# Second attention: the exchange of the rotation's halves moves from two extra projections to a VectorE shuffle

## The reference, cut to what matters

```
def _apply_rope(x, cos, sin):
    d2 = x.shape[-1] // 2
    x1, x2 = (x[..., :d2], x[..., d2:])
    return jnp.concatenate([x1 * cos - x2 * sin, x2 * cos + x1 * sin], axis=-1)
qkv = x @ Wqkv.T + bqkv
qkv = qkv.reshape(b, t, 3, NHEAD, HEAD_DIM).transpose(2, 0, 3, 1, 4)
q, k, v = (qkv[0], qkv[1], qkv[2])
q = _apply_rope(q, cos, sin)
k = _apply_rope(k, cos, sin)
attn = jax.nn.softmax(jnp.einsum('bhqd,bhkd->bhqk', q, k) / scale, axis=-1)
out = jnp.einsum('bhqk,bhkd->bhqd', attn, v)
return out.transpose(0, 2, 1, 3).reshape(b, t, d) @ Wout.T + bout
```

## Time and profile before

| | |
|---|---|
| time, median of 3 runs (lowest to highest) | 2202.04 us (2201.79 to 2204.19) |
| span of the profiled execution, first to last instruction | 2190.9 us |
| busy, share of the span: PE, DVE, ACT, POOL | 73%, 57%, 49%, 37% |
| second attention, first statistics to last pick | about 1396 to 1914 us of the span |

### The profile page before, as it was taken

The page is one execution under the profiler, slowest core; times in us unless marked ns, Lnnn a source line. Parts: engine busy times, 40 slices in busy tenths (PEclk is TensorE's granted clock), DMA queues, the critical chain, the costliest instruction groups (busy, mean ns, idle before and its releaser), DMA issues. The chain is left out here.

```text
span 2190.9 us, 25810 instructions
## 1 busy us (share of the span) xinstructions
PE 1588.8 (73%) x8422; PEld 824.9 (38%) x8422; DVE 1256.8 (57%) x2743; ACT 1080.2 (49%) x2160; POOL 819.4 (37%) x1482
## 2 busy tenths in 40 slices
PE   2799999963498851615530179159999999879998
PEld 1133333312365640513430157013333333357776
DVE  3688888856434230154468721368777778435443
ACT  1377777755333330246650022217777776645554
POOL 3455554325334235270061776533344431012111
PEclk8699999985655555857755579559999999979999
DMA  3211212100000021100003113211111111010000
GB/s 97 73 66 61 70 67 67 45 1 1 1 1 1 1 81 51 30 7 1 0 3 116 39 39 28 49 72 55 57 57 58 60 52 52 12 40 10 6 10 15
DMA packets 85097, 85.19 MB, mean 39 GB/s; under 512 B 36070, under 2 KB 67664, under 8 KB 84836
## 3 DMA queue, kind: packets, MB, share of 16 engines
q1 hardware_dynamic: 75044, 76.43, 10.5%
q0 software_dynamic: 7680, 6.06, 1.7%
q10 hardware_dynamic: 2240, 1.05, 0.2%
HBM read 59.78 MB, written 25.17 MB: 39 GB/s over the span
## 5 line engine op out<-in xcount | busy, mean ns | idle before, releaser
L921 DVE TENSOR_REDUCE arena<-psum 128x2 f32<-128x1024 f32 x512 | 602.1, 1218 | 131.1 <-PE psum L720 126.4
L836 ACT ACTIVATE arena<-psum 128x512 f32<-128x512 f32 x1024 | 554.1, 595 | 141.0 <-PE psum L733 131.9
L733 PE MATMUL psum<-arena 99*128 99x512 bf16 x1024 | 312.6, 387 | 16.4 <-DMA arena<-arena 11.8
L720 PE MATMUL psum<-arena 72*128 72x512 bf16 x1024 | 287.5, 397 | 43.0 <-POOL arena L622 20.8
L743 PE MATMUL psum<-arena 128*32 128x512 f32 x2048 | 274.3, 608 | 3.0 <-ACT arena L836 1.9
L733 PEld LDWEIGHTS psum<-arena 99*128 99x128 bf16 x1024 | 74.8, 98 | 294.0 <-ACT arena L836 224.7
L720 PEld LDWEIGHTS psum<-arena 72*128 72x128 bf16 x1024 | 96.7, 102 | 185.6 <-DVE arena L921 28.5
L2406 ACT ACTIVATE arena<-arena 128x128 f32<-128x128 f32 x252 | 102.5, 482 | 110.5 <-POOL arena L2394 110.5
L2389 POOL TENSOR_SCALAR arena<-arena 128x4 f32<-128x4 f32 x80 | 22.3, 278 | 307.5 <-DVE arena L2383 302.7
L631 POOL TENSOR_TENSOR arena<-arena 128x16 bf16<-128x16 f32 x64 | 13.8, 216 | 317.6 <-DVE arena L921 223.3
L344 ACT ACTIVATE arena<-arena 128x128 f32<-128x128 f32 x192 | 76.7, 482 | 96.2 <-POOL arena L260 70.9
(11 more groups left out here) (436 smaller groups left out, 2647.6 us busy)
## 6 DMA issues: line engine op xcount, KB each, us to landing
arena<-L_q_parts SPq DMA_DIRECT2D x192, 96.0 KB
arena<-L_k_parts SPq DMA_DIRECT2D x192, 96.0 KB
L_q_parts<-arena SPq DMA_DIRECT2D x16, 384.0 KB, 3.3
L_k_parts<-arena SPq DMA_DIRECT2D x16, 384.0 KB, 3.2
arena<-in_L_ffn_w SPq DMA_DIRECT2D x1, 2048.0 KB, 10.7
ec_result<-arena SPq DMA_DIRECT2D x1, 2048.0 KB
arena<-in_L_ffn_fc2s SPq DMA_DIRECT2D x1, 2048.0 KB, 16.4
ec_normed<-arena SPq DMA_DIRECT2D x1, 2048.0 KB
```

Source lines behind the costliest of these rows:

```text
L720: last = nc.tensor.matmul(bank[:, 512 * h:512 * h + 512], columns(q9[0:QK_ROWS], i, m // 2, 128 * (2 * (m % 2) + h), 128), columns(k9[0:QK ...
L733: nc.tensor.matmul(acts.bank(name), columns(k9[0:ROWS], i, g, 128 * k, 128), columns(q9[0:ROWS], i, g, 0, 512), start=True, stop=True).the ...
L836: nc.scalar.activation(prob[:, k % 2, g, :], acts.bank(name), ACT.Exp, scale=scale).then_inc(act_taken, 1)
L921: nc.vector.tensor_reduce(neg_max[:, i % 2, 2 * m:2 * m + 2], maxes.bank(("max", i, m)).rearrange("p (h t) -> p h t", h=2), axis=AX.X, op= ...
```

## The change

The second pair of projections, its weights `w_swap` and its biases go away. In their place VectorE makes `other` from `full` by a `stream_shuffle`, which exchanges partitions 0 to 15 with 16 to 31 in each group of 32. `split_parts` waits for it. In the steady state the shuffle stands in part 1 of the third (q) and fourth (k) quad of a group, behind that part's two `take`s. At the stage's start the four shuffles of batches 0 and 1 stand ahead of VectorE's two `operand`s.

```
 def items(b):
-    swap = lambda kind: ((kind, b), (kind + "_swap", b)) if rope else ((kind, b),)
-    return {"n": (("n", b),), "q": swap("q"), "k": swap("k"), "v": (("v", b),)}
+    return {kind: ((kind, b),) for kind in "nqkv"}
...
 def split_parts(eng, ch, b, n):
...
     if rope:
+        eng.wait_ge(exchanged[n], b + 1)
         ch.mark(eng.tensor_tensor(f, f, cos_t, ALU.mult))
...
 def queries(b):
     project(("q", b), w_qk[:, 0, :])
-    if rope:
-        project(("q_swap", b), w_swap[:, 0, :])
 def keys(b):
     project(("k", b), w_qk[:, 1, :])
-    if rope:
-        project(("k_swap", b), w_swap[:, 1, :])
...
 def keep(b, n):
...
         nc.scalar.activation(full[:, n, :], acts.bank(name), ACT.Identity, bias=qk_bias[:, n:n + 1]).then_inc(act_taken, 1)
-        act.wait_ge(act_made, acts.count(swap))
-        nc.scalar.activation(other[:, n, :], acts.bank(swap), ACT.Identity, bias=qk_bias[:, 2 + n:3 + n]).then_inc(act_taken, 1)
...
 def order_weights():
...
-    nc.vector.tensor_copy(halves(w_swap)[:, :, 0, :], halves(w_qk)[:, :, 1, :])
-    nc.vector.tensor_copy(halves(w_swap)[:, :, 1, :], halves(w_qk)[:, :, 0, :]).then_inc(swapped, 1)
...
+def exchange(b, n):
+    dve.wait_ge(act_taken, acts.count(("qk"[n], b)))
+    if b >= 1:
+        dve.wait_ge(part_done[n], b)
+    nc.vector.stream_shuffle(other[:, n, :], full[:, n, :], list(range(16, 32)) + list(range(16))).then_inc(exchanged[n], 1)
...
-operand(0, 0)
-operand(1, 0)
+for b in range(AHEAD):
+    if rope:
+        exchange(b, 0)
+        exchange(b, 1)
+    operand(b, 0)
...
             if i + 2 < QUADS:
                 take(i + 2, 2 * k)
                 take(i + 2, 2 * k + 1)
+            if rope and i // TPB + AHEAD < B and k == 1 and r >= 2:
+                exchange(i // TPB + AHEAD, r - 2)
```

More of the change, by code:

```diff
@@ L477, in attention_layer @@
         qk_bias, v_bias, cos_t, sin_t, select = tables.qk_bias, tables.v_bias, tables.cos, tables.sin, tables.select
-        w_swap = c.take(256).rearrange("p (w c) -> p w c", w=2)
         other = both()
-        swapped, summed, picked = sem("swapped"), sem("summed"), sem("picked")
+        exchanged = [sem("q_exchanged"), sem("k_exchanged")]
+        summed = sem("summed")
         fetched = [sem(f"fetched{b}") for b in range(B)]
@@ L756, in _ @@
             pe.wait_ge(ordered, 1)
-            if rope:
-                pe.wait_ge(swapped, 1)
             for b in range(AHEAD):
@@ L816, in keep @@
                 if rope:
-                    swap = name[0] + "_swap", b
                     nc.scalar.activation(full[:, n, :], acts.bank(name), ACT.Identity, bias=qk_bias[:, n:n + 1]).then_inc(act_taken, 1)
-                    act.wait_ge(act_made, acts.count(swap))
-                    nc.scalar.activation(other[:, n, :], acts.bank(swap), ACT.Identity, bias=qk_bias[:, 2 + n:3 + n]).then_inc(act_taken, 1)
                 else:
@@ L892, in order_weights @@
                 last.then_inc(ordered, 1)
-                if rope:
-                    dve.wait_ge(ordered, 1)
-                    halves = lambda m: m.rearrange("p w (t two f) -> p (w t) two f", two=2, f=16)
-                    nc.vector.tensor_copy(halves(w_swap)[:, :, 0, :], halves(w_qk)[:, :, 1, :])
-                    nc.vector.tensor_copy(halves(w_swap)[:, :, 1, :], halves(w_qk)[:, :, 0, :]).then_inc(swapped, 1)
             def o_spread(b):
@@ L2659, in laid_out @@
     bias = np.asarray(inputs["L3_attn_bqkv"])[0:2 * D].reshape(2, 4, 4, 2, HD // 2)
-    columns = [b.transpose(0, 1, 3, 4, 2).reshape(2, D) for b in (bias, bias[:, :, :, ::-1, :])]
-    return {"qk_bias": np.concatenate(columns).T, "choice_gate": np.asarray(inputs["L2_ffn_gate_w"]).T}
+    return {"qk_bias": bias.transpose(0, 1, 3, 4, 2).reshape(2, D).T, "choice_gate": np.asarray(inputs["L2_ffn_gate_w"]).T}
 class RotaryTables:
     def __init__(self, c):
-        self.qk_bias = c.take(4)
+        self.qk_bias = c.take(2)
         self.v_bias = c.take(D)
```

## The result

The changed kernel took 2208.3 us (2204.2 to 2213.2, 18 runs) against 2202.9 us (2201.5 to 2205.6, 18 runs) for the kernel before: ratio 1.0021, 95% interval 1.0014 to 1.0028. That is slower by 3 to 6 us, where 5.9 us less were forecast. A later comparison of the same two gave 1.0014, interval 1.0004 to 1.0023.

A forecast was written before the change was run, and what follows sets the result against it. TensorE's stream was taken to bound the second attention. Projections -10.3, start +3.9 and VectorE's addition +0.5 gave -5.9 us, from 2202.0 to 2196.1; its own range was 2194.1 to 2201.2, with rivals (b) and (c) 2192 to 2201.5.

The forecast's parts named there:

- What bounds the kernel, and the projections that go: Second attention: TensorE's stream sets the pace; 12 dropped projections on its path save 0.86 us each, 10.3 us less.
- The shuffle in the steady state: VectorE, third and fourth quads: a shuffle takes about 0.71 us, 0.75 with the gap, and is free up to 1.12 us.
- (a): Rival, chance 0.07: the shuffle is long and VectorE takes the maxima late; a loss from 1.49 us per exchange.
- (b): Rival, chance 0.15: VectorE becomes the bound in third and fourth quads; half of the 10.3 may be lost, 2201.3 us.
- GpSimd's later rotation: Third and fourth quads: GpSimd starts behind the shuffle, fits by 2.5 and 0.6 us; SyncE's store and load 5 to 8 later.
- (d): Rival, chance 0.08: the 8 bytes' shift of later tiles changes DMA or engine-read pace in any stage; 2 us either way.
- VectorE's addition beside GpSimd's rotation: Third quad: VectorE's 0.68 us addition now meets GpSimd's rotation, 0.94 more as at the start; costs 0.5 us in all.
- The stage's start: Second attention's start: k's rotation waits for VectorE's shuffles, so k's store, first load and first maximum tile come 3.9 us later.
- the upper bound: Stage's start at worst: shuffles of 1.22 us each and nothing regained ahead of them make it 6.3 us later.
- (c): Rival, chance 0.10: the start costs nothing, absorbed by the first load's landing or second batch's loads; 10.3 us less, 2191.7.
- Strict turns: Stage's start: each of GpSimd's seven operations waits for a 0.6 us VectorE operation, 4.2 us more; sum 2.7 us worse.
- The accounting of the level: Whole kernel: profiled span 2190.9 us, the runs' median 11.1 above it, a gap taken to lie outside what changes.

The follow-up runs named there:

- the second profile: The changed kernel profiled again with no edit; measured 2209.8 us, span 2208.0.
- the last experiment: Changed kernel, with the load of a group's third quad put behind the next row maxima and the store left in place: 2238.5 us, ratio 1.0143.
- the second pair of profiles: Both kernels run and profiled again with no edit: 2206.2 us for the kernel before (span 2204.7), 2209.8 us for the changed one (span 2208.0).
- The second shuffle of the experiment: Kernel with SyncE's load ahead of its store, plus another, unread shuffle behind each of twelve steady ones: second turn to last 404.9 us; no total given.

## Why the prediction was wrong

The time lies outside the range and on the other side of no change. Step by step:

- **What bounds the kernel, and the projections that go.** Right. Each quad with a projection lost 0.86 to 0.88 us; with the wait removed the stretch shrank by 10.9 us against 10.3 forecast.
- **The shuffle in the steady state.** Right: 0.72 us for 0.71, the cover about 1.17 for 1.12, and no loss. Rivals (a) and (b) are out, and GpSimd's later rotation costs nothing by itself: with the load ahead of the store the distances are 13.70 to 13.73. Rival (d), the addresses, is not seen, within about 2 us. The separate load of the lane table that the Trainium skill names ("Vector Engine (DVE) Microarchitecture Reference", 3.8) is there, at 0.014 us.
- **VectorE's addition beside GpSimd's rotation.** It took 1.71 us in all five steady quads for 0.68, as the start's 1.62 foretold, but the quad with k was 13.72 long all the same: the 0.5 us of the sum were 0.
- **The stage's start.** Right: 3.8 us later for 3.9 forecast, with two small errors that cancel. GpSimd's seven operations took 9.15 us beside VectorE, 8.7 forecast, so k's store went out 4.2 us later than before, counted from the reload; but the first load then followed it by 2.74 us and not by 3.33. (The 6.3 of the upper bound comes to 6.2 from its own terms.) Rival (c) is out. Strict turns by the Trainium skill ("SBUF — State Buffer", Who interferes with whom) would have made them 11.4; GpSimd lost 1.95 us instead of 4.2, and VectorE, with 3.7 us, lost more.
- **The step that failed** is the sentence at the end of "GpSimd's rotation, later": "SyncE's store and the load behind it come 5 to 8 us later, but that load is needed more than a quad afterwards." It asked only when the moved instructions' own results are needed. It did not ask what stands behind them on SyncE's queue. That is the DMA of the row maxima, which the trace before has 0.57 us behind each turn (1635.41 for the turn at 1634.85 in the earlier trace rows), with some 6 us until TensorE needs it. The load's issues pushed it 1.0 us back and its data lay in front of it: 10.1 us of TensorE's waits in the steady part (9.2 in the second profile), which is about the gain of all twelve projections. The 5 to 8 us for the delay were right. The reason given was wrong as well, though nothing came of it here: the load is needed some 12 us after it now goes out, less than a quad, and the last experiment shows what a further delay costs.
- **The accounting of the level.** The forecast was tied to a profile 13 us short of what the program mostly does, and the gap of 11.1 us between its span and the median was taken for surroundings. They are 1.9 us. This did not harm the difference, but it would have harmed any share worked out from the stages ahead.

Taking the second pair of profiles, the change is +3.8 us at the start, -0.7 to the second turn, -2.4 in the steady part (with an odd quad in before's), -1.0 behind it and +3.6 ahead of the second attention, together +3.3. Within the second attention and behind it that is -0.3, no change, so in the profiles the slower result rests on the last figure. The expert stage began at 1268 to 1270 us in seven profiles and at 1273 to 1274 in five. The two kinds part between 700 and 900 us, far ahead of the change, and they differ there in the granted clock. Over 700 to 758 us it was 0.59 in all seven early ones and 0.53 to 0.56 in the five late ones (before, then after):

```profile
700.00:758.00 58.00, 46.92 (x196) 32.77 (x195) 18.35 (x77) 21.20 (x59) 19.97 (x43) 0.59 0.00 1
700.00:758.00 58.00, 47.35 (x183) 33.15 (x182) 17.89 (x76) 21.32 (x59) 19.18 (x40) 0.56 0.00 1
```

The four profiles with the old addresses are all early; of the eight with the new ones five are late and three early. Whether the change makes the late one more likely is not settled by so few; the interval of the total has room for either.

## What to carry to other kernels

When an instruction moves later on an engine, follow everything that is queued behind its consumers, down to the DMA queue, and ask of each when it is needed: a small transfer on which the pacing engine waits every few microseconds must not stand behind a large one that nobody needs yet. Here one exchange of two calls in SyncE's stream turned a loss of 0.1 to 0.2% into a gain of 0.4%. With two shuffles moved ahead of a memset as well it was 0.6%; the profiles show this second gain, while the two totals' intervals overlap. And compare a profile's span with the median of the runs: if the gap is larger than in sister runs, the profiled execution was not a typical one.

## What the runs showed of the hardware

- A 12 KB transfer took 6.4 to 7.0 us from issue to TensorE's start with 576 KB issued just ahead of it, its packets running some 5.4 to 5.9 us after the issue (twice to 6.5). With the load moved behind they ran at 1.4 to 1.6 us. Another queue did not free it: 4.1 to 6.7 us.
- VectorE operations on 128x512 float32 with two SBUF inputs took 0.98 to 1.71 us beside GpSimd's instead of 0.68, and so did casts with one input: 1.20 to 1.37 instead of 0.43. GpSimd's 1.09 us operations took up to 1.54.
- A shuffle, also with one input, was 0.715 to 0.735 us wherever it stood first. The second shuffle of the experiment ran beside the start of GpSimd's L507 and took 0.74 to 0.75, L507 its usual 1.09 to 1.10.
- Shuffles back to back start 0.63 us apart, 0.1 less than one's own 0.72.
- In the last experiment TensorE waited six times for about 3 us, in a stretch that otherwise runs at full clock. Its granted clock was at half for 3 to 14 us after each wait, which cost about as much as the waits: 17 us beside 18.7.
- In the expert stage the engines lose about 13 us to waits that the profile puts down to issue, in eleven of twelve profiles, all but the first; the cause is open.
